# Matmuls without a reader at the beginning of six stages of a two-layer transformer kernel

## What is computed

```python
def reference(...):
    x = L0_attn_x                                       # 4 x 1024 x 256
    x = x + 0.5 * _L0_ffn_ref(_layernorm(x), ...)       # expert layer
    x = x + _L0_attn_ref(_layernorm(x), ...)            # causal softmax attention, 16 heads
    x = x + 0.5 * _L0_ffn_ref(_layernorm(x), ...)       # expert layer, the same weights
    x = x + 0.5 * _L1_ffn_ref(_layernorm(x), ...)       # FP4 feed-forward
    x = x + _L1_attn_ref(_layernorm(x), ...)            # linear attention
    x = x + 0.5 * _L1_ffn_ref(_layernorm(x), ...)       # FP4 feed-forward, the same weights
    return x

def _L0_ffn_ref(x, W_router, W1, b1, Wo, bo, gamma, beta):   # 4 experts, inner width 1024
    expert_idx = argmax(x @ W_router)
    h = gelu(x @ W1[expert_idx] + b1[expert_idx])
    return layer_norm(h @ Wo + bo + x) * gamma + beta

def _L1_ffn_ref(x, w_gate, w_up, w_down):                    # inner width 704
    h = silu(fp4_linear(x, w_gate)) * fp4_linear(x, w_up)
    return fp4_linear(h, w_down)        # fp4_linear rounds both operands in blocks of 16
```

## Times and profile before

| | |
|---|---|
| median of 3 runs | 2276.48 us (2274.24 to 2277.07) |
| profiled execution | 2266.27 us, span 2264.6 us |
| PE (TensorE matmul) busy | 2037.3 us, 90% of the span |
| DVE (VectorE) busy | 1448.9 us, 64% |
| ACT (ScalarE) busy | 1021.6 us, 45% |
| POOL (GpSimd) busy | 921.9 us, 41% |
| mean granted TensorE clock | 0.962 |

### The profile page before, as it was taken

The page is one execution under the profiler, slowest core; times in us unless marked ns, Lnnn a source line. Parts: engine busy times, 40 slices in busy tenths (PEclk is TensorE's granted clock), DMA queues, the critical chain, the costliest instruction groups (busy, mean ns, idle before and its releaser), DMA issues. The chain is left out here.

```text
span 2264.6 us, 41707 instructions
## 1 busy us (share of the span) xinstructions
PE 2037.3 (90%) x13665; PEld 1410.6 (62%) x13665; DVE 1448.9 (64%) x3940; ACT 1021.6 (45%) x2367; POOL 921.9 (41%) x1143
## 2 busy tenths in 40 slices
PE   6699994989999999987899975999979999699998
PEld 6599992534444444356899973666656666467676
DVE  4342224768888888626674227998757666588885
ACT  4233331416666666744333322333326666433332
POOL 5222226621111111116122236666546666455553
PEclk9999996989999999997899997999999999899999
DMA  5465552554444444012555642000000000000000
GB/s 172 146 202 193 196 180 79 177 109 57 57 58 57 57 55 52 10 39 75 189 185 200 195 138 61 14 14 9 1 1 2 2 2 2 2 10 10 19 19 19
DMA packets 101709, 173.56 MB, mean 77 GB/s; under 512 B 14704, under 2 KB 66320, under 8 KB 101520
## 3 DMA queue, kind: packets, MB, share of 16 engines
q1 hardware_dynamic: 95376, 154.40, 26.2%
q0 software_dynamic: 6144, 16.79, 2.3%
HBM read 136.01 MB, written 34.87 MB: 75 GB/s over the span
## 5 line engine op out<-in xcount | busy, mean ns | idle before, releaser
L1106 DVE TENSOR_REDUCE a_part_max<-a_psS 128x1 f32<-128x512 f32 (+3 forms) x608 | 362.6, 655 | 79.3 <-PE a_psS L1036 70.7
L1162 ACT ACTIVATE a_PT<-a_psE 128x512 f32<-128x512 f32 (+1 forms) x608 | 309.3, 584 | 179.0 <-PE a_psE L1050 162.0
L577 PE MATMUL e_psH<-e_xsT,e_w 128*128 128x128 f32 x2240 | 265.8, 278 | 0.0
L577 PEld LDWEIGHTS e_psH<-e_xsT,e_w 128*128 128x128 f32 x2240 | 260.2, 195 | 0.1
L586 PE MATMUL e_psY<-wo_moe,e_gT 128*128 128x256 f32 x1120 | 253.0, 380 | 0.0
L1011 POOL TENSOR_SCALAR_AFFINE_SELECT a_PT<-a_PT 128x512 f32<-128x512 f32 x128 | 81.2, 634 | 409.2 <-ACT a_PT L1162 409.2
L1030 PE MATMUL a_psS<-sk,sq 96*128 96x512 bf16 (+3 forms) x768 | 232.7, 338 | 13.0 <-DMA sk<-qk_parts 8.2
L1050 PE MATMUL a_psE<-sq,sk 98*128 98x512 bf16 (+3 forms) x768 | 224.7, 330 | 4.1 <-DMA sq<-a_maxT 1.8
L586 PEld LDWEIGHTS e_psY<-wo_moe,e_gT 128*128 128x128 f32 x1120 | 207.9, 191 | 25.1
L608 ACT ACTIVATE e_gT<-e_psH,e_bias 128x128 f32<-128x128 f32 x560 | 159.6, 368 | 137.4 <-PE e_psH L577 134.4
L656 POOL TENSOR_TENSOR e_rstd<-e_moments,minus_half 128x1 f32<-128x1 f32 x70 | 45.2, 646 | 408.7 <-DVE e_moments L122 408.7
(11 more groups left out here) (295 smaller groups left out, 3781.4 us busy)
## 6 DMA issues: line engine op xcount, KB each, us to landing
e_w<-w_in SPq DMA_DIRECT2D x70, 1024.0 KB, 5.0
sq<-qk_parts SPq DMA_DIRECT2D x96, 128.0 KB, 6.0
sk<-qk_parts SPq DMA_DIRECT2D x96, 128.0 KB, 6.6
e_xs<-sorted_x SPq DMA_DIRECT2D x70, 128.0 KB, 2.0
e_xr<-sorted_x SPq DMA_DIRECT2D x70, 128.0 KB, 4.1
sorted_y<-e_yo SPq DMA_DIRECT2D x70, 128.0 KB, 1.7
X<-x_in SPq DMA_DIRECT2D x8, 512.0 KB, 6.4
qk_parts<-q_hi SPq DMA_DIRECT2D x32, 128.0 KB, 1.7
```

The lines of the kernel that those rows point to most:

```text
L577: mm = pe.matmul(psH[p][:, n * P:(n + 1) * P], w1[p][:, k, n * P:(n + 1) * P], xsT[p][:, k, :], start=k == 0, stop=k == KD - 1)
L1106: dve.tensor_reduce(part_max[:, c, h0:h0 + heads, qt], psS[place % RING][:, 0:heads * n].rearrange("p (h k) -> p h k", h=heads), AX.X, ALU ...
L1162: act.activation(PT[kt % 2][:, h0:h0 + heads, q0:q0 + n], psE[e % RING][:, 0:heads * n].rearrange("p (h q) -> p h q", h=heads), ACT.Exp, s ...
```

## The change

At the beginning of TensorE's program in six stages the new function `keep_warm` runs a fixed number of matmuls of the bf16 mask `hide_k_after_q` (repeated four times, 512 columns) with `ident_bf` as weights, into a PSUM bank of the stage that its real work overwrites later. Nobody reads the result, and no semaphore is raised. The numbers are 14 in e0 and e1, 45 in q, 70 in f0, 20 in f1 and 8 in l. In f0 and f1 they stand ahead of the wait for `padded`. Nothing else changes.

```diff
+def keep_warm(pe, bank, st, passes):
+
+    for _ in range(passes):
+        pe.matmul(bank[:, 0:512], st.ident_bf[:], st.hide_k_after_q[:].unsqueeze(1).broadcast_to([P, 4, P]),
+                  start=True, stop=True)
@@ -555,6 +562,7 @@
         @block.tensor
         def _(pe):
+            keep_warm(pe, psY[0], st, 14)
 
             def turn(t, p):
                 pe.wait_ge(x_in[p], 8 * (t - p) + 16)
@@ -816,6 +824,8 @@
         @block.tensor
         def _(pe):
+            keep_warm(pe, psQ[0], st, 45)
+
             def turn(g, p):
@@ -1508,6 +1518,7 @@
         @block.tensor
         def _(pe):
+            keep_warm(pe, psGate, st, 70 if gathers else 20)
             pe.wait_ge(padded, 2)
@@ -1797,6 +1808,8 @@
         @block.tensor
         def _(pe):
+            keep_warm(pe, psQ, st, 8)
+
             def pair(t, p):
```

## The result

| | before | after |
|---|---|---|
| median | 2274.92 us (13 runs, 2273.27 to 2277.07) | 2269.18 us (13 runs, 2267.76 to 2274.71) |
| ratio | | 0.9978, 95% interval 0.9971 to 0.9985 |
| profiled execution | 2266.27 us, span 2264.6 | 2269.09 us, span 2267.4 |
| PE busy | 2037.3 us, 13665 matmul records | 2080.9 us, 13836 |

The kernel became 0.22% faster: 5.0 us by the ratio (3.4 to 6.6), against the 4.90 us of the forecast. The gain is certain as to its sign.

The account below looks back on a forecast made before the run. TensorE was taken to bound the expert stages, whose entries ran at the lower clock. Gains of 2.05 us (e0) and 2.85 us (e1), nothing elsewhere, sum to 4.90 us: 2276.48 to 2271.6 us, range 2268 to 2277.5 us.

Parts of the forecast that it names:

- The passes: In e0 and e1, 14 passes take 4.3 to 6.0 us, at 0.43 us each cold and 0.22 us warm.
- the rows' bounds of 2.5 and 5.9 us: Dense TensorE work before the clock rises: 2.5 us in the linear attention, 5.9 us in e1.
- e0 and e1: Second transposes start as before and run warm with the up projection; gains 2.05 us in e0, 2.85 us in e1.
- The release of e0: Barrier that frees e0's engines, put at 78.1, 2.89 us ahead of the first transposes as in e1.
- The second weights: In e0, tile two's weights land at 89.2, still 0.4 us ahead of the earlier up projection at about 89.6.
- q, f0 and f1: Passes end too early, idle 4.1 to 5.7, 5.4 to 7 and 6.4 us; clock lost, nothing gained.
- The linear attention: 8 passes leave 2.0 us idle; counted as 0 gained, with 0 to 1.6 us in the range.
- Rival 1: Clock falls again in the gap after the passes in e0, e1 or both; 2273.6 to 2276.5 us, chance 0.27.
- that stretch up to 3.4 us: In e0 and e1, time without work as the clock sees it, if transposes don't count as busy.
- a do-nothing edit: Passes warm nothing, or weights landing at 89.2 and ScalarE's table load set the ramp; 2276.5 us, chance 0.09.
- "same": Whole kernel: change within about 0.2% (4.55 us), not measurably different from none; chance 0.55.
- rival 4: f0's 70 passes stay cold and hold up its first transposes by 6.4 us; 2282.9 us, chance 0.07.

Follow-up runs that it names:

- filled: Changed kernel with passes lengthened to 70 in q, 98 in f0, 49 in f1, 16 in the linear attention; 2260.41 us, ratio 0.9964 to before.
- f0_over: Changed kernel with 120 passes in f0 instead of 70; 2261.93 us, ratio 0.9968 to before.
- gap_again: The same kernel as filled_gap, run once more; 2256.09 us, ratio 0.9948 to before.
- e_twenty: Changed kernel with 20 passes instead of 14 in e0 and e1 and none elsewhere; 2262.57 us, ratio 0.9977 to before.
- after_again: The changed kernel, unchanged, under a new name for a second profile; 2259.82 us, ratio 0.9966 to before.
- rest_only: Changed kernel without the passes in e0 and e1, keeping those in q, f0, f1 and the linear attention; 2266.63 us, ratio 0.9993 to before.
- before_again: The kernel before, unchanged, under a new name for a second profile; 2267.76 us, ratio 0.9993 to before.
- e_six: Changed kernel with 6 passes instead of 14 in e0 and e1 and none elsewhere; 2266.93 us, ratio 0.9992 to before.
- filled_gap: filled with 15 further passes in q behind the first group's transposes; 2256.63 us, ratio 0.9951 to before.

## Why the prediction came out right, point by point

- The passes. From the first of 14 to the first transposes it took 4.30 us (filled and f0_over, e1) to 5.92 us (f0_over, e0), against 4.3 to 6.0 predicted. A warm pass costs what the 0.22 us of the mask matmul said: 49 passes in f1 under a full clock took 10.73 us (filled), 0.215 us each from start to start. The time until the rise varies as much as the rows' bounds of 2.5 and 5.9 us did: 2.6 us in gap_again (4.33 us for 14 are some six passes at 0.43 and eight at 0.215), 5.9 us in e_twenty (7.23 us for 20 are 13.6 slow ones). The Trainium skill, TensorE: Matmul & The Clock Gate, says in Part 1, under What's actually happening, that the number of matmuls that run cold at the start differs from run to run for the same kernel. These profiles agree: the same 14 passes of the same kernel took 5.09 us in e1 in after and 4.56 us in after_again.
- e0 and e1. The release of e0 was put at 78.1 and is 78.05 to 78.11, by the first pass, in all profiles but after's. The second transposes didn't move for the passes: with 14 they start at 85.43 to 85.54 us in all profiles but after's, against 85.62 before. The stretch from them to the next ones is 3.84 us or so where the clock held (before 5.84), and 4.07 us in e1 (before 6.86). The gains reach the end of both stages: 2.1 us in e0, and in e1 2.4 us behind the start of the up projection and 0.4 us ahead of it, together 2.8, against 2.05 and 2.85 predicted. The second weights were in time: TensorE's second up projection follows the transposes at once.
- q, f0 and f1. Predicted idle times behind the passes: 4.1 to 5.7, 5.4 to 7 and 6.4 us; measured 5.48, 6.22 and 6.32 us. The clock was lost in all three, and rest_only's q, f0 and f1 gained nothing.
- The linear attention. Predicted 2.0 us of idle time, measured 1.86 us, and the clock fell at about 1679.6 (0.82 in its slice), just ahead of the projection at 1679.81. It was counted at 0 with 0 to 1.6 us in the range. After's profile bears out the 0, but by luck of the draw: two of four profiles with 8 passes held the clock over the same idle time. And the bound of 1.6 us was too low, since not only the projection is cold without passes: in before_again the two steps behind it are too (0.63 and 1.66 us against 0.38 and 1.03), and a warm entry shortens the ramp by 1.4 to 3.1 us.
- Rival 1 happens in e0 and e1, but seldom: one entry of 14, and on purpose in e_six. The transposes' part in it stays open. After the passes filled_gap lost the clock across 2.7 us (83.13 to 85.81) with two pairs of transposes in it, and gap_again held it across 3.3 us with the same pairs; by the length of the stretch without dense work alone the longer one would have been the likelier to fall, so this pair decides nothing about the transposes. The prediction called that stretch up to 3.4 us; by its own times it is 3.7 us in e0 (82.4 to 86.10) and 3.6 us in e1, and the longest measured, in gap_again's e1, was 3.47 us, held.
- What was off. The chances: I gave rival 1 0.27 and a do-nothing edit 0.09, and "same" 0.55, when 13 of 14 entries held the clock. The linear attention, as said. And rival 4 was priced one to one with its overrun, when f0_over, with passes that ended warm, gave back 3.4 of 5.0 us.
- What was luck. The mechanism in e0 and e1 is shown stage by stage, but that 4.90 us met 5.0 so closely is not: the interval is 3.4 to 6.6 us, and the same kernel gained 7.7 us (4.3 to 11.1) in after_again's job (0.9966).
- What stays open: the "remote" waits in after's routing stages; what decides whether the clock survives a gap of 1.9 to 2.7 us; why filled_gap's linear attention is 3 us longer behind its entry; and why after's ratio is 0.9978 in one job and 0.9966 in another, whose intervals overlap. In the stages that the edit touches the two profiles of after differ by 0.8 us in e0 (after is shorter) and by 1.2 us in the linear attention (after is longer, its clock was lost there). If after's clock is lost at that entry in some executions and not in others, its times must scatter by about as much; how often it is, two profiles can't tell.

## What to carry to other kernels

Look for dense TensorE stages whose first real matmuls run at half speed behind a barrier or a wait for a load; the price of the cold start is the difference between the first and the second step of equal work, and matmuls on data at hand, put into the idle time, buy it back. They pay only if the clock outlives what is left of the idle time, so count them from the release to the first work. Here it did so in 13 of 14 entries with 1.04 to 2.67 us left, and in none with 3.8 us or more. Whether an overrun of a fraction of a microsecond beats ending early these runs can't tell: 20 passes were no better than 14. A single profile doesn't decide about such an entry either, since the same kernel was seen on both sides. Where another engine sets the pace behind the entry, as in f0, a warm start gains nothing. And when stages are compared by the starts of their first matmuls, look at when these start too: passes that overrun make the stretch behind them shorter, which is no gain.

## What the runs showed of the hardware

The granted clock can rise after six matmuls of 0.43 us and be at its lower level again after 3.85 us of idle time, before any dense real work has used it (e_six, e1). Around 2 us of idle time its fate is not fixed by the program: the same kernel lost it behind 1.96 us in one execution and kept it over 2.67 us in another (filled_gap and gap_again, e0), and the linear attention's entry, behind 1.85 to 1.86 us and a further 0.47 us, lost it in after and f0_over and kept it in rest_only and after_again. The fall can come when work has resumed: 0.2 us after it in filled_gap's e0, 0.6 us after it at 1662.80 in before. At 3.78 and 3.85 us (e_six) and at 5.5 us and more it was lost each time. A stage held up by 5.0 us of useless matmuls ended only 1.6 us later, since the other engines kept working meanwhile and the rest of TensorE's ramp ran at the full clock (f0_over).
